# Routing in half the head pairs, the expert bias on VectorE, and block loads on another queue, in a transformer block with 160 routed experts

## The reference

```
h = layernorm(x) * (1 + ca) + sa                          # ca, sa, ... per batch
x = x + ga * attention(h)                                 # 16 heads of 64, bias by relative position
h = layernorm(x) * (1 + cb) + sb
probs = sigmoid(h @ router_w.T + expert_bias)             # 160 experts
top_w, top_idx = top_k(probs, 8);  top_w = 2.5 * top_w / (sum(top_w) + 1e-9)
routed = sum over the 8 chosen e of top_w[e] * silu(h @ w_gate[e].T) @ w_down[e].T
x = x + gb * (routed + silu(h @ w_gate_shared.T) @ w_down_shared.T)
```

## Time and profile before

| | |
|---|---|
| median of 3 runs | 912.48 us (906.68 to 912.83) |
| profiled execution | 911.5 us, span 909.7 us |
| busy: PE, DVE, ACT, POOL | 797.6, 551.8, 471.7, 542.1 us |
| transfers | 174.13 MB, mean 191 GB/s |
| attention of batch 0, with what stands ahead of it | to 146.70 us |
| attention of batches 1 to 3 | 146.70 to 533.26 us |
| from there to the first block transpose | 533.26 to 611.59 us |
| expert steps | 611.59 to 760.40 us |
| dense rest, gathers, end | 760.40 to 909.70 us |

### The profile page before, as it was taken

One profiled execution on the slowest core, in us unless ns is written; L12 is line 12 of the kernel. 1 busy time (PEld: TensorE's weight loads), 2 busy tenths in 40 slices (PEclk: granted clock), 3 DMA queues, 4 the chain that ended last, 5 costly groups with the idle time before them and its releaser, 6 DMA issues.

```text
span 909.7 us, 14260 instructions
## 1 busy us (share of the span) xinstructions
PE 797.6 (88%) x4442; PEld 501.9 (55%) x4442; DVE 551.8 (61%) x1386; ACT 471.7 (52%) x975; POOL 542.1 (60%) x418
## 2 busy tenths in 40 slices
PE   4889989999999999999889888809999889988882
PEld 2656656666666666566556555407777655433331
DVE  5867666766677777767776756304444333565755
ACT  3666656666766557776667841204554433323220
POOL 0588878897788877778656772650000002877774
PEclk9899999999999999999999988758999988999996
DMA  7976966757666553553543865759999986777762
GB/s 233 241 204 194 275 183 189 184 164 184 186 157 191 143 113 76 134 139 90 124 112 92 254 221 209 230 182 344 289 311 313 314 273 193 180 164 182 177 152 58
DMA packets 80878, 174.13 MB, mean 191 GB/s; under 512 B 12434, under 2 KB 30292, under 8 KB 78500
## 3 DMA queue, kind: packets, MB, share of 16 engines
q1 hardware_dynamic: 69860, 143.51, 56.9%
q0 software_dynamic: 6144, 12.60, 5.1%
q10 hardware_dynamic: 4800, 17.11, 4.9%
HBM read 96.75 MB, written 45.48 MB: 156 GB/s over the span
## 4 chain that ended last, share of the span: by engine, by line
PE 46%; POOL 16%; DVE 11%; issue 10%; ACT 9%; DMA 5%; SPq 2%; DVEq 0%; POOLq 0%; ACTq 0%
POOL wT L1367 11%; PE ps L643 9%; PE ps L630 9%; ACT prob L1095 4%; PE ps L593 4%; POOL sorted_rows L1325 4%; PE ps L956 3%; PE ps L619 3%; DMA wT<-sorted_rows 3%; PE ps L621 3%; PE ps L996 3%; PE ps L978 3%; DVE prob L1483 3%; PE ps L656 2%; PE ps L1022 1%
## 5 line engine op out<-in xcount | busy, mean ns | idle before, releaser
L1309 POOL TENSOR_SCALAR prob<-prob,rinv 128x512 f32<-128x512 f32 x215 | 336.0, 1573 | 112.2 <-DVE rinv L1501 110.0
L1095 ACT ACTIVATE prob<-prob,nmax 128x512 f32<-128x512 f32 x256 | 183.0, 716 | 147.4 <-DVE nmax L1483 146.4
L1367 POOL DMA_INDIRECT wT<-sorted_rows,dest x96 | 104.9, 1093 | 188.6 <-DMA sorted_rows<-prob 159.6
L343 DVE COPY PT<-ps 128x512 f32<-128x512 f32 x128 | 88.2, 689 | 132.1 <-PE ps L630 131.1
L1483 DVE CUSTOM_DVE_ANT_0 prob<-ps,strips 128x512 f32<-128x512 f32 x256 | 164.8, 680 | 1.3 <-PE ps L621 0.6
L630 PEld LDWEIGHTS ps<-ident,prob 128*128 128x128 f32 x1024 | 114.2, 141 | 80.2 <-POOL prob L1309 42.7
L630 PE MATMUL ps<-ident,prob 128*128 128x128 f32 x1024 | 136.8, 276 | 6.8 <-ACT PT L343 4.0
L643 PE MATMUL ps<-PT,v_sb 128*64 128x512 f32 x512 | 126.0, 614 | 7.8 <-ACT PT L343 7.6
L619 PE MATMUL ps<-stack 128*128 128x512 f32 x256 | 113.4, 443 | 4.0 <-DVE nmax L1483 3.7
L1325 POOL DMA_INDIRECT sorted_rows<-xn,dest x96 | 95.7, 996 | 34.8 <-issue 34.8
L1231 ACT ACTIVATE strips<-ps 128x512 f32<-128x512 f32 x80 | 47.8, 597 | 111.1 <-PE ps L1015 111.1
(11 more groups left out here) (267 smaller groups left out, 1194.3 us busy)
## 6 DMA issues: line engine op xcount, KB each, us to landing
stack<-qk SPq DMA_DIRECT2D x128, 256.0 KB, 3.9
sorted_rows<-in_zero_rows SPq DMA_DIRECT2D x16, 1024.0 KB, 5.6
wT<-sorted_rows SPq DMA_DIRECT2D x32, 512.0 KB, 6.0
sorted_rows<-prob ACTq DMA_DIRECT2D x22, 512.0 KB, 5.0
qk<-comb_rows SPq DMA_DIRECT2D x40, 256.0 KB, 4.8
strips<-in_expert_rows SPq DMA_DIRECT2D x96, 96.0 KB, 2.7
k_low<-qk SPq DMA_DIRECT2D x64, 128.0 KB, 3.6
hT<-qk SPq DMA_DIRECT2D x64, 128.0 KB
```

What stands on the lines that cost most here:

```text
L343: return copy(dst[:, :, qt * P:(qt + 1) * P], ps[:, BANK_T + u % 2, :].rearrange("p (k s) -> p k s", s=P))
L1095: nc.scalar.activation(prob[:, u, :], prob[:, u, :], ACT.Exp, bias=nmax[:, u:u + 1], scale=-1.0, accum_out=rsum[:, u:u + 1]).then_inc(s_ex ...
L1309: nc.gpsimd.tensor_scalar(prob[:, u, :], prob[:, u, :], rinv[:, u:u + 1], None, ALU.mult).then_inc(s_prob, 1)
L1367: nc.gpsimd.indirect_dma_start(picked[:, n % NGATHER, k, :], None, sorted_rows, bass.IndirectOffsetOnAxis(ap=dest[:, n, k:k + 1], axis=0)) ...
```

## The change

- The routing of a batch lies in the pairs 2 to 8 (batch 1: to 9) of the next batch, so that batch 2's also ends within attention, in pair 31. Transposes and logits take pairs 3 and 4, the counts pair 5, the bases and the first ranks pair 6 (batch 1: 7), the others the next pair. A projection bank is used two or three times in such a pair. `destinations` of batch 2 is in the second part of pair 31.
- The expert bias is no longer a product with a row of ones on TensorE (L680), but an addition by VectorE; one sigmoid per batch takes the place of two.
- Normalising moves: ScalarE helps from pair 17 on instead of 21, and from 26 instead of 28; in pair 31 POOL does one unit. Scatters of batch 0 are in the pairs 17 to 24, of batch 1 in 26 to 30; of batch 2, twelve come ahead of the power operation for batch 3's deviation.
- After attention the shared expert comes first; TensorE does batch 3's router without batch 2's counts, ranks and block table.
- In the steps ScalarE issues the block loads after the first six; SP keeps the chosen loads (a whole step's at once) and the spreads. Three chosen sets instead of four precede the first blocks. 10 dense pairs lie beside the steps, not 15.
- The zeroing of the sorted list goes from one fill per pair to two in batch 1.

```
-BESIDE = 15
+BESIDE_STEPS = range(2, NSTEPS, 3)
+BESIDE = len(BESIDE_STEPS)
-FIRST_SCATTER, SECOND_SCATTER = 2 * HPAIRS + 5, 3 * HPAIRS + 4
+FIRST_SCATTER, SECOND_SCATTER = range(17, 25), range(26, 31)
+LAST_PAIR = B * HPAIRS - 1
...
 def normaliser(pair, u):
-    if pair < FIRST_SCATTER:
+    if pair < FIRST_SCATTER[0]:
         return ON_POOL
-    if pair < SECOND_SCATTER:
+    if pair < SECOND_SCATTER[0]:
         return ON_ACT if u in (1, 3, 7) else ON_POOL
-    return ON_ACT if u % 2 == 1 else ON_DVE if u == 2 else ON_POOL
+    if pair < LAST_PAIR:
+        return ON_ACT if u % 2 == 1 else ON_DVE if u == 2 else ON_POOL
+    return ON_POOL if u == 0 else ON_DVE if u in (2, 4) else ON_ACT
...
+            load_known(14)
+            load_known(15)
+            load_known(16)
+            load_known(18)
+            for k in range(NCHOSEN - 1):
+                load_chosen(k)
             sp.wait_ge(s_scatter, 16 * TILES * TOPK)
             for s in range(NX):
-                load_blocks(s)
+                first, _ = STEPS[s]
+                sp.dma_start(x_blocks[:, s, :, :], block_rows[:, first:first + STEP, :]).then_inc(s_x[s], 16)
+            load_chosen(NCHOSEN - 1)
...
             for s in range(NSTEPS):
-                load_blocks(s + NX)
...
-                for late_by, blocks in ((2, range(0, 3)), (3, range(3, 6)), (4, range(6, 8))):
-                    if s - late_by in CHOSEN:
-                        load_chosen(CHOSEN.index(s - late_by) + NCHOSEN, blocks)
-                if s >= 8 and s % 4 == 0:
-                    load_spread(s // 4 - 2 + NROWS)
+                if s in CHOSEN:
+                    load_chosen(CHOSEN.index(s) + NCHOSEN)
+                if s >= BESIDE_STEPS[1] + 2 and (s - BESIDE_STEPS[1] - 2) % 6 == 0:
+                    load_spread(next(spreads))
...
+            def route_first(b, n):
+                now, bank, bases = b - 1, BANK_PROJ + n % 2, bases_pair(b - 1)
+                if n == 3:
+                    unused(b, n)
+                    transpose_normed(now, bank)
+                elif n == 4:
+                    unused(b, n)
+                    logits(now, 1, bank)
+                elif n == bases:
+                    unused(b, n)
+                    sum_blocks(now, bank)
+                elif n == bases + 1 and b < LAST:
+                    unused(b, n)
+                    rank(now, 1, bank)
+                elif n == bases + 1:
+                    pe.wait_ge(s_by_dve, routed(now, RANKED1))
+                    blocks_before()
+            def route_second(b, n):
+                if n == 3:
+                    logits(now, 0, bank)
+                elif n == 4:
+                    pe.wait_ge(s_added, 2 * now + 2)
+                    transpose_back(now, bank)
+                elif n == bases_pair(now):
+                    pe.wait_ge(s_by_dve, routed(now, BASED))
+                    rank(now, 0, bank)
+            def route_third(b, n):
+                if n == 5:
+                    unused(b, n)
+                    count(now, BANK_PROJ + n % 2)
+                elif b == LAST and n == bases_pair(now):
+                    pe.wait_ge(s_vc, B * HPAIRS)
+                    rank(now, 1, BANK_PROJ + 1)
...
             copy_transposed(0)
+            load_blocks(NX)
             for s in range(NSTEPS):
                 block_silu(s)
...
                 if s >= 1:
                     copy_results(s - 1)
+                load_blocks(s + 1 + NX)
                 beside(s)
...
-            scatter_more(1, SCATTERS)
-            invert_deviation(B - 1)
-            scatter(2, 0, SCATTERS)
+            scatter(2, 0, 12)
+            invert_deviation(LAST)
+            scatter(2, 12, SCATTERS)
...
+            def add_expert_bias(b, half, bank):
+                dve.wait_ge(s_logits, 2 * b + half + 1)
...
+                nc.vector.tensor_tensor(
+                    probs[b][:, 2 * half:2 * half + 2, :], ps[:, bank, 0:2 * E].rearrange("p (n e) -> p n e", e=E),
+                    bias_all[:, :].rearrange("p (o e) -> p o e", o=1).broadcast_to([P, 2, E]), ALU.add).then_inc(s_added, 1)
```

More of the change, by code:

```diff
@@ L859, in pair @@
                     transpose_probs(b, n - 1, 5)
+                if b >= 1 and n >= 2:
+                    route_first(b, n)
                 scores(b, n, 2)
@@ L880, in pair @@
                     attend(b, n - 1, 1)
+                if b >= 1 and n >= 2:
+                    route_third(b, n)
                 transpose_probs(b, n, 0)
@@ L1147, in pair @@
                     copy_probs(b, n - 1, 4)
+                act_bank[0] = BANK_PROJ + n % 2
+                if b >= 1 and n == 3:
+                    modulate(b - 1)
                 exponential(b, n, 2)
@@ L1172, in pair @@
                 copy_probs(b, n, 0)
+                if b >= 1 and n == 4:
+                    copy_back(b - 1)
                 exponential(b, n, 6)
@@ L1236, in _ @@
             copy_gate_rows()
+            copy_shared_rows(0)
+            shared_silu(0)
+            copy_shared_rows(1)
             act_bank[0] = MODULATE_BANK
             modulate(LAST)
-            copy_shared_rows(0)
-            for half in range(2):
-                act_bank[0] = LOGIT_BANKS[half]
-                sigmoids(LAST, half)
-            shared_silu(0)
-            copy_shared_rows(1)
-            copy_comb()
+            sigmoid(LAST)
             shared_silu(1)
@@ L1248, in _ @@
             shared_silu(2)
+            copy_comb()
             shared_silu(LAST)
@@ L1788, in pair @@
             def pair(b, n, final=False):
-                now, before = b - 1, b - 2
-                dve_bank[0] = BANK_PROJ + n % 2
                 add_bias(b, n, 0)
@@ L1805, in pair @@
                 invert_sums(b, n, 0)
-                if now >= 0 and n == 6:
-                    top(now, 1)
-                elif now >= 0 and n == 7:
-                    top(now, 3)
-                elif now >= 0 and n == 8:
-                    mask(now)
-                if before >= 0 and n == 3:
-                    top_keys(before, 0)
-                elif before >= 0 and n == 4:
-                    top_keys(before, 2)
-                elif before >= 0 and n == 5:
-                    index_keys(before, 1)
+                if b >= 1 and n >= 2:
+                    route(b, n, 1)
                 add_bias(b, n, 2)
@@ L1890, in pair @@
                     qk_low(b, n + 2)
-                if now >= 0 and n == 5:
-                    top(now, 0)
-                elif now >= 0 and n == 6:
-                    top(now, 2)
-                elif now >= 0 and n == 9:
-                    scale_top(now)
-                if before >= 0 and n == 2:
-                    keep_keys(before, 0)
-                elif before >= 0 and n == 3:
-                    keep_keys(before, 1)
-                    top_keys(before, 1)
-                elif before >= 0 and n == 4:
-                    index_keys(before, 0)
+                if b >= 1 and n >= 2:
+                    route(b, n, 4)
             dve_bank = [0]
@@ L2046, in route_table @@
     table[:, 0:P] = lane[:, None] < lane[None, :]
-    table[0, 128:288] = expert + 1
+    table[0:32 * SORTED:32, 128:288] = expert + 1
     table[:, 288:448] = lane[:, None] < expert[None, :]
```

384 lines of the change are left out of this document (195 added, 189 removed).

## The result

The changed kernel takes **898.88 us** (median of 4 runs, 898.01 to 902.46) against 911.94 before (4 runs, the three shown above and one more), a ratio of 0.9876 (0.983 to 0.9922): 1.2%, clear of the noise but under 2%. The profiled execution has a span of 896.2 us, 13.5 less than before. The forecast was 870, with 852 to 895 as its range: the sign was right, two thirds of the gain are missing.

The account below looks back on a forecast made before the run. Bounds: TensorE in attention and steps (plus block-load waits), POOL and SP together at the hand-over, POOL in the gathers. Terms 4.5 - 28.1 - 18.8 + 1.0 = -41.4 gave span 868.3, time 870 us, range 852 to 895.

Parts of the forecast that it names:

- Attention: Attention of batches 1 to 3: routing and what goes with it costs 51.0 us instead of 46.5, a change of +4.5 us.
- fifteen loaded pairs: Attention, pairs 3 to 7 of each next batch: 3.4 us each above a clean pair, between 2.6 and 4.7, 51.0 in all.
- light rests in the neighbours: Attention, pairs beside the fifteen loaded ones: small remaining routing work, given no price of its own in the sum.
- VectorE's idle third as cover: Attention: bias additions, two per batch, hide in VectorE's idle time (busy 9.6 of 14.17 us); uncovered they cost 3 us.
- rival 1: Attention pays in full: loaded pairs cost 4.7 us each through TensorE waits for VectorE, 71 instead of 51, total 890; chance 0.16.
- Hand-over: Attention's end to the first block transpose: it starts at 583.5 instead of 611.59, -28.1 us.
- SP was next: Hand-over: SP's chosen loads end at 576.9, 1.6 us before POOL, so a faster POOL gains no more than that.
- Steps: The 32 expert steps take 130 us instead of 148.81, -18.8 us, bounds 125 and 137.
- start-up and slower clock: Expert steps: 10.8 us beyond TensorE's work and block-load waits, kept on top of 119.9 to give 130.7.
- The second reading: Expert steps: the stage's 44.6 MB at the busiest slice's rate, 344 GB/s, take 129.8 us.
- Gathers: Last part: POOL's 133.7 us cover five more dense pairs, which only stretch a few gathers, +1 us.
- the 20 that the prediction named as the sign: Attention: the forecast is wrong if TensorE's waits for VectorE before q/k projections grow beyond 20 us.

Follow-up runs that it names:

- the probe with three insertions: Changed kernel, five small VectorE fills at three parts of clean pairs: ahead of bias additions (pairs 3, 4) 30.59 against 28.33 us, behind (8, 9) 28.85 against 28.85.
- The kernel before with this half of the change: Kernel before plus block loads on ScalarE's queue, whole chosen sets on SP and ten dense pairs, routing unchanged: 886.94 us, ratio 0.9743.
- the last kernel: Changed kernel with zero fills apart, tangent for sigmoid, VectorE's routing behind bias additions and seventeen early scatters: 853.66 us, ratio 0.9372.
- the probe with one insertion: Changed kernel, eight small VectorE fills in one part of pairs 3 and 8: pairs 3 and 4 together grew 0.5 us, pair 8 by 0.55.
- the fills apart: Changed kernel with the two 1 MB zero fills ahead of the next batch's token load moved to other pairs: 885.07 us.

## Why the prediction was wrong

- **Attention: the failed step.** The sum priced fifteen loaded pairs, at 3.4 us each between bounds of 2.6 and 4.7, and put the nine other pairs, its "light rests in the neighbours", at nothing: 51.0 us above clean pairs. Measured were 81.3. By the places listed above, the fifteen (n = 3 to 7) take 59.1 of them, 3.9 each, or 3.5 without the 5.9 us of fills in pair 14; so the price was right as a mean, though n = 4, with two routing steps and the sigmoid, took 6.0 and n = 3 took 1.8. The nine (n = 2 and the first two pairs of a batch) take the other 22.2. They are not light, as the pairs 10 and 24 show:

```profile
178.63:195.59 16.96, 16.11 (x92) 10.33 (x88) 13.39 (x42) 9.47 (x22) 14.95 (x11) 1.00 0.64 172
424.61:443.41 18.80, 17.78 (x102) 11.64 (x99) 13.22 (x36) 11.31 (x25) 12.79 (x10) 1.00 0.47 114
```

  VectorE is busy there for 13.4 and 13.2 us, against 9.62 in a clean pair. In the kernel before the same nine pairs already took 15.4 us more than clean ones. What the sum had no term for at all is the place: moving VectorE's operations alone gave 30.3 us back, 10.2 of them in the nine pairs and 20.1 in the fifteen. The probes fit this (one insertion of 2.0 us cost 0.5, so a pair has some 1.5 us of slack; three ahead of the bias additions cost 2.3); that each routed pair pays in this way was not traced.
- **VectorE's idle third as cover.** The prediction hid the expert bias's additions in it (9.6 of 14.17 us), and held it against rival 1. The idle time is there, but right behind the position bias additions, and the routing stood ahead of the next ones: the probe with three insertions cost 2.3 us in one place and none in the other. What the expert bias's additions cost by themselves no run shows.
- **An edit left without a price.** The zero fills, two per pair in batch 1, were told in the change and not costed. They stood ahead of the next batch's load and cost 5.9 us in pair 14.
- **The sigmoid** was counted as a saving (two table loads instead of four). In one piece of 3.34 us it is late for two exponentials and for the bank's copy; without its table loads the attention took 5.2 us less.
- **Batch 0** has the same code but for one small load and took 3.1 us longer: 1.1 at the start and 1.6 in pair 6, where a wait of 2.40 instead of 2.34 us was followed by products at half clock. It differs between executions (146.7 to 150.7 us in the kernels that share that code).
- **Hand-over: right.** -25.1 for -28.1; the missing 3.0 are POOL's one long gap, 5.46 instead of 2.42 us. SP was next, as said.
- **Steps: right in mechanism, too small in size.** -24.6 for -18.8. The waits for blocks are gone and above TensorE's 119.9 us of work 4.4 are left, not the 10.8 that were kept for start-up and slower clock. The second reading took the busiest slice, 344 GB/s, as the pace; the changed steps moved 356. The waits had been put at 8.5 us. The kernel before with this half of the change reached the first gather 20.2 us sooner, and five dense pairs beside the steps cost 11.2 (forecast 9.6), so the queue and the order of the loads were worth some 9.0 there by difference. The 21.3 us of block loads on SP, 16.0 of them waits for blocks, belong to a list with eight chosen loads ahead of a block load.
- **Gathers: right within 3 us.** 135.1 us of gathers, -1.8 for the stretch where +1.0 was forecast.

Rival 1 had the right stretch with too low a price, +24 in its sum and +35 measured, and not the mechanism: TensorE's waits for VectorE ahead of the q/k projections are 3.2 us in all, far from the 20 that the prediction named as the sign. The longest in sum are those for ScalarE's copies ahead of the products with the values, 15.5 us.

What stays open: why single executions of one kernel differ by 5 to 10 us in the steps and gathers (128.6 to 131.7 and 135.0 to 141.4 us in the kernels with the new loads on ScalarE's queue, the new routing and ten dense pairs), and the hand-over of the old routing by 4 (73.9 to 78.3); no run here was made on it. How much of the remaining 43 us above clean pairs is TensorE's own routing work was not measured apart either: by the row of the last kernel TensorE is busy for 25.8 of them and idle for 16.9, but its busy time also fell by 11.4 us when VectorE's operations alone were moved.

## What to carry to other kernels

Price every iteration that the moved work touches, the light ones too: here nine pairs that were put at nothing held 22.2 us. Idle share is no cover by itself: ask where in the loop an engine is idle, and put added work there, behind the instruction that feeds the next engine and ahead of the one that waits for data. Don't price several insertions in one iteration as a multiple of one: in the probe here the slack covered the first, and the others were paid. And look at every load that stands behind a large transfer on the same queue, also when the large one is only moved.

## What the runs showed of the hardware

TensorE's six projection products ran at half clock (2.8 to 2.9 us) behind waits of 2.40, 2.45 and 5.30 us in the changed kernel, and behind 2.15 us in the probe with one insertion. They ran at full clock (1.65 to 1.66 us) behind 2.34 us in the kernel before, behind 2.43 and 2.55 with VectorE's routing moved, and behind 2.45 with the fills apart. A load of 512 KB issued behind two fills of 1 MB landed after 9.0 us, and after 4.4 without fills ahead of it.
